# The first graph's set-up rebuilt in a graph network with experts, 16 graphs on one core

## The reference

```
H  = (adj != 0);  w = adj's first row
Be = 1 / column sums of H;  Dn = 1 / (H @ w)
conv(x, W, b) = Dn * (H @ (Be * (H.T @ (x @ W.T)))) + b
h  = relu(conv(layernorm(x), W1, b1))            # 512 wide
h  = layernorm(h) * gamma + beta
x1 = x + conv(h, W2, b2) + layernorm(x)          # 256 wide
x2 = layernorm(x1)
p  = softmax of the top 2 of 4 router logits of x2
e  = sum over experts of p * silu(x2 @ ew + eb)
y  = x2 + e @ ow + ob
out = x1 + nw * y / rms(y)
```

## Time and profile before

| what | value |
|---|---|
| time, median of 3 runs | 728.39 us (727.57 to 728.85) |
| the profiled execution's own time | 727.07 us |
| its span, first to last instruction | 725.5 us |
| TensorE busy | 685.5 us (94%) |
| VectorE busy | 622.0 us (86%) |
| ScalarE busy | 530.5 us (73%) |
| GpSimd busy | 345.2 us (48%) |
| the chain that ended last | PE 87%, DVE 5%, ACT 3% |

### The profile page before, as it was taken

One profiled execution on the slowest core, in us unless ns is written; L12 is line 12 of the kernel. 1 busy time (PEld: TensorE's weight loads), 2 busy tenths in 40 slices (PEclk: granted clock), 3 DMA queues, 4 the chain that ended last, 5 costly groups with the idle time before them and its releaser, 6 DMA issues.

```text
span 725.5 us, 15868 instructions
## 1 busy us (share of the span) xinstructions
PE 685.5 (94%) x5197; PEld 475.7 (66%) x5197; DVE 622.0 (86%) x1542; ACT 530.5 (73%) x1096; POOL 345.2 (48%) x732
## 2 busy tenths in 40 slices
PE   3777999999999999999999999999999999999973
PEld 2464485866758586775858577685857668585663
DVE  3987799898989989898989989898998989898676
ACT  4567868688696868778686877869686786967554
POOL 4142635456373545636354454635455463634444
PEclk9999999999999999999999999999999999999998
DMA  8547449375664938666583946657494756538312
GB/s 285 189 79 241 91 111 246 78 236 117 212 139 134 231 66 247 121 209 137 152 204 61 276 97 226 121 167 180 73 263 98 231 116 195 123 72 190 59 30 59
DMA packets 42590, 111.72 MB, mean 154 GB/s; under 512 B 4160, under 2 KB 5312, under 8 KB 42560
## 3 DMA queue, kind: packets, MB, share of 16 engines
q0 software_dynamic: 13536, 41.42, 32.5%
q1 hardware_dynamic: 29024, 69.92, 27.6%
HBM read 69.91 MB, written 16.25 MB: 119 GB/s over the span
## 4 chain that ended last, share of the span: by engine, by line
PE 87%; DVE 5%; ACT 3%; DMA 1%; issue 1%; POOL 1%; SPq 0%; POOLq 0%; DVEq 0%; ACTq 0%
PE bank L1335 16%; PE bank L1337 16%; PE bank L1336 16%; PE bank L1420 7%; PE bank L1421 7%; PE bank L1446 7%; PE bank L1478 4%; PE bank L1479 4%; PE bank L1389 4%; PE bank L1382 2%; PE bank L1437 2%; DMA b1b<-b 1%; PE bank L1491 1%; PE bank L1370 0%; ACT x L598 0%
## 5 line engine op out<-in xcount | busy, mean ns | idle before, releaser
L1335 PE MATMUL bank<-xth,ewh 128*128 128x512 f16 (+1 forms) x270 | 99.6, 369 | 2.6 <-DVE ewl L840 2.6
L1337 PE MATMUL bank<-xth,ewl 128*128 128x512 f16 (+1 forms) x270 | 99.8, 370 | 0.0
L1336 PE MATMUL bank<-xtl,ewh 128*128 128x512 f16 (+1 forms) x270 | 99.6, 369 | 0.0
L543 ACT ACTIVATE silu<-bank,ebcol,ksc 128x512 f32<-128x512 f32 x120 | 89.6, 768 | 7.7 <-POOL comb L400 3.9
L400 POOL TENSOR_TENSOR comb<-comb,silu 128x1024 f32<-128x1024 f32 x30 | 74.6, 2488 | 0.6 <-DVE silu L917 0.6
L1335 PE MATMUL bank<-w2h,hnth 128*128 128x256 f16 x256 | 70.3, 275 | 0.6 <-issue 0.6
L1336 PE MATMUL bank<-w2l,hnth 128*128 128x256 f16 x256 | 70.4, 275 | 0.0
L1337 PE MATMUL bank<-w2h,hntl 128*128 128x256 f16 x256 | 70.4, 275 | 0.0
L939 DVE SCALAR_TENSOR_TENSOR hntl<-bank,hnth 128x512 f16<-128x512 f32 x64 | 42.7, 687 | 26.6 <-ACT hnth L561 25.2
L1478 PE MATMUL bank<-xsh,h 128*128 128x256 f16 x256 | 59.4, 280 | 2.9 <-DVE xsl L822 2.3
L917 DVE TENSOR_TENSOR silu<-silu,bank 128x1024 f32<-128x1024 f32 x45 | 54.7, 1216 | 8.2 <-ACT silu L543 8.2
(11 more groups left out here) (283 smaller groups left out, 2077.1 us busy)
## 6 DMA issues: line engine op xcount, KB each, us to landing
adjin<-adj SPq DMA_DIRECT2D x16, 1024.0 KB, 5.4
adjtin<-adjt SPq DMA_DIRECT2D x16, 1024.0 KB, 8.2
xin<-x SPq DMA_DIRECT2D x16, 512.0 KB, 7.8
xb<-xn SPq DMA_DIRECT2D x16, 512.0 KB, 4.2
xb<-x POOLq DMA_DIRECT2D x16, 512.0 KB, 8.9
xb<-b POOLq DMA_DIRECT2D x16, 512.0 KB, 5.4
xb<-vadd POOLq DMA_DIRECT2D x16, 512.0 KB, 4.5
out<-x SPq DMA_DIRECT2D x15, 512.0 KB, 4.9
```

What stands on the lines that cost most here:

```text
L543: af(silu[:, i % 4, :], bank[E_BANK[i]][:, :], ACT.Silu, bias=ebcol[:, i:i + 1], scale=ksc[:, 2:3]).then_inc(silu_dn, 1)
L1335: mm(outp, lh, rh, start=first, stop=False)
L1336: mm(outp, lh, rl, start=False, stop=False)
L1337: return mm(outp, ll, rh, start=False, stop=last)
```

## The change

Loads: adj, W1 and adj transposed come right behind x; gamma, W2, beta and b1 follow as one group, and W1 has a semaphore of its own.

Magnitudes: ScalarE now writes the sum of the absolute values of a row straight into `mags` (`sum_abs`) for W1, gamma*W2 and the experts, in place of an absolute value whose maximum VectorE takes. VectorE takes the maximum itself for the two small matrices of group c. GpSimd multiplies gamma by W2.

Degrees: of graphs 0 and 1, TensorE adds them up by 16 products of H with a column of ones (`count_products`); graph 0's H transposed is one instruction of VectorE. From graph 2 on ScalarE counts them, as before.

Order in graph 0: x is normalised and split in two halves of two tiles, and A1 starts with the first half (`first_aggregation`); W1 is scaled before the second half of A1 is copied; Dn is computed before A2 is split; `beta_w2` follows the products with W1; GpSimd's `dnb` waits for group b apart from `dna`. TensorE multiplies zeros before its first real product (18 products of 512 columns) and between two transposes (twice 5), in `keep_busy`. Order in graph 1: the expert weights' halves are made earlier, those of the output weights later.

VectorE's program has 12 small memsets (`PAD`) in front of everything else. The loop's own code is as before except for the constants that the semaphores are compared with.

```diff
-            for dst, src in ((bet[:, :], beta), (gam[:, :], gamma),
+            sp.dma_start(adjin[:, :, :], adj[0].rearrange("(t p) e -> p t e", p=P)).then_inc(adj_in, 16)
+            sp.dma_start(w1f[:, :, :], w1t.rearrange("(k p) h -> p k h", p=P)).then_inc(a_in, 16)
+            sp.dma_start(adjtin[:, :, :], adjt[0].rearrange("(t p) c -> p t c", p=P)).then_inc(adjt_in, 16)
+            for dst, src in ((gam[:, :], gamma), (w2f[:, :, :], w2t.rearrange("(k p) f -> p k f", p=P)),
+                             (bet[:, :], beta), (b1b[:, :], b1.to_broadcast([P, DH]))):
...
+            gp.wait_ge(b_in, 64)
+            tt(w2g[:, :, :], w2f[:, :, :], gam[:, :].unsqueeze(2).to_broadcast([P, KH, D]), ALU.mult).then_inc(w2g_dn, 1)
...
+            def sum_abs(col, src):
+                n = src.shape[1] * src.shape[2]
+                return af(silu[:, :, :].rearrange("p k n -> p (k n)")[:, 0:n], src[:, :, :].rearrange("p k n -> p (k n)"),
+                          ACT.Abs, accum_out=mags[:, col:col + 1])
+
+            def first_x():
+                act.wait_ge(xrs_st, 4)
+                for j in range(2):
+                    s = slice(CG * j, CG * j + CG)
+                    for t in range(CG * j, CG * j + CG):
+                        af(xn[:, t, :], xin[:, t, :], ACT.Identity, bias=xnb[:, t:t + 1],
+                           scale=xrs[:, t:t + 1]).then_inc(xn_dn, 1)
+                    act.wait_ge(xn_dn, CG * j + CG)
+                    af(xsh[:, s, :], xn[:, s, :], ACT.Copy, scale=XS).then_inc(xs_hi if j else x0_hi, 1)
 
             def bias_rows(act, g):
...
+            for i in range(PAD):
+                v.memset(lead[:, i:i + 1], 0.0)
...
-            def first_ht():
-                dve.wait_ge(adjt_in, 16)
-                for t in range(CT):
-                    TS(ht16[0][:, t, :], adjtin[:, t, :], 0.0, None, ALU.not_equal, ALU.add,
-                       accum_out=deg[:, t:t + 1]).then_inc(ht_made, 1)
-                dve.wait_ge(ht_made, CT)
...
+            def first_lo(j):
+                s = slice(CG * j, CG * j + CG)
+                dve.wait_ge(xs_hi if j else x0_hi, 1)
+                STT(xsl[:, s, :], xn[:, s, :], XS, xsh[:, s, :], ALU.mult, ALU.subtract).then_inc(xs_lo if j else x0_lo, 1)
+
+            def setup_w1l(k):
+                dve.wait_ge(a_hi, 1)
+                STT(w1l[:, k, :], w1f[:, k, :], wsc[:, W1:W1 + 1], w1h[:, k, :], ALU.mult, ALU.subtract).then_inc(a_lo, 1)
...
+            def keep_busy(n):
+                for _ in range(n):
+                    mm(bank[7][:, :], m16[:, 0, :], m16[:, :, :].rearrange("p t c -> p (t c)"), start=True, stop=True)
+
+            def count_products():
+                for e in range(CT):
+                    for k in range(CT):
+                        ins = mm(bank[DEG_BANK][:, DEG][:, e:e + 1], h16[:, k, P * e:P * e + P], one16[:, :],
+                                 start=(k == 0), stop=(k == CT - 1))
+                ins.then_inc(deg_rdy, 1)
+
+            def first_aggregation():
+
+                def part(e, ks):
+                    b = bank[A1_BANK[e // CG]][:, D * (e % CG):D * (e % CG) + D]
+                    for k in ks:
+                        mm(b, h16[:, k, P * e:P * e + P], xsh[:, k, :], start=(k == 0), stop=False)
+                        ins = mm(b, h16[:, k, P * e:P * e + P], xsl[:, k, :], start=False, stop=(k == CT - 1))
+                    return ins
+
+                pe.wait_ge(x0_lo, 1)
+                part(0, (0, 1))
+                part(CG, (0, 1))
+                pe.wait_ge(xs_lo, 1)
+                part(0, (2, 3))
+                part(1, range(CT)).then_inc(a1_rdy, 1)
+                turn_mags(a_mag, 1, slice(W1, W1 + 1), 0, a_turn)
+                part(CG, (2, 3))
+                spread_max(a_top, 1, 0, a_max)
+                part(CG + 1, range(CT)).then_inc(a1_rdy, 1)
+
+            def first_product():
+                b = bank[A3_BANK[0]][:, :]
+                for k in range(KD):
+                    pe.wait_ge(a2_hi, k + 1)
+                    mm(b, a2h[:, k, 0:P], w1h[:, k, :], start=(k == 0), stop=False)
+                    pe.wait_ge(a_lo, k + 1)
+                    mm(b, a2h[:, k, 0:P], w1l[:, k, :], start=False, stop=False)
+                for k in range(KD):
+                    pe.wait_ge(a2_lo, k + 1)
+                    ins = mm(b, a2l[:, k, 0:P], w1h[:, k, :], start=False, stop=(k == KD - 1))
+                ins.then_inc(a3_rdy, 1)
 
             def a2_half(g, odd, half, ffn):
...
-                    setup_lo(c_hi, 2, ((rwf, rwh, rwl, RW), (owf, owh, owl, OW)), c_lo)
+                    setup_lo(c_hi, 1, ((rwf, rwh, rwl, RW),), c_lo)
...
+                    setup_lo(c_hi, 2, ((ewf, ewh, ewl, EX),), c_lo)
...
-                    setup_hi(c_scale, ((rwf, rwh, RW), (owf, owh, OW)), c_hi)
+                    setup_hi(c_scale, ((rwf, rwh, RW), (ewf, ewh, EX), (owf, owh, OW)), c_hi)
...
+            pe.wait_ge(tables, 12)
+            keep_busy(18)
```

More of the change, by code:

```diff
@@ L421, in body @@
                         root(hstat, hmv, hve, hrs, hnm, hnb, hrs_st, g, 16, 4 * t, slice(t, t + 1), 4, t + 1)
+                        if not ffn and t == 1:
+                            add_b2(g)
                 if ffn:
@@ L604, in body @@
                     a1_part(act, g, odd, 0)
+                if conv and not ffn:
+                    setup_hi(a_scale, ((w1f, w1h, W1),), a_hi)
                 if ffn:
@@ L608, in body @@
                     a1_part(act, g, odd, 1)
-                if conv and not ffn:
-                    setup_hi(a_scale, ((w1f, w1h, W1),), a_hi)
+                    if not ffn:
+                        act.wait_ge(a_mag, 1)
+                        act.wait_ge(w2g_dn, 1)
+                        sum_abs(W2, w2g).then_inc(b_mag, 1)
                 if ffn:
                     x2_part(act, f, 1)
-                if conv and ffn and not late:
-                    setup_hi(c_scale, ((ewf, ewh, EX),), c_hi)
                 if ffn:
@@ L658, in body @@
                     expert(act, f, 3)
+                if conv and not ffn:
+                    setup_hi(b_scale, ((w2g, w2h, W2),), b_hi)
                 if conv:
                     norm_h(act, g, 1)
+                if conv and not ffn:
+                    hnt_part(act, g, 0)
+                    relu(act, g, 3)
+                    hnt_part(act, g, 1)
                 if ffn:
@@ L695, in body @@
                         if e % CG == 0:
+                            if not ffn and e == 0:
+                                prep_x(g + 1, (0, 1))
                             act.wait_ge(u_rdy, 2 * g + e // CG + 1)
@@ L1062, in body @@
                 if conv and ffn:
-                    degrees(g, odd)
+                    degrees(g, odd, not late)
                 if ffn:
@@ L1097, in body @@
                 if conv and ffn and not late:
-                    setup_lo(c_hi, 3, ((ewf, ewh, ewl, EX),), c_lo)
+                    setup_lo(c_hi, 3, ((owf, owh, owl, OW),), c_lo)
                 if conv and ffn:
@@ L1463, in body @@
                 if conv:
-                    if not ffn:
-                        beta_w2()
                     pe.wait_ge(h_made, g + 1)
@@ L1469, in body @@
                         pe.wait_ge(y_dn, 2 * (g - 1))
-                    pe.wait_ge(xs_lo, g + 1)
-                    for e in range(CT):
-                        if ffn and e == 0:
+                    else:
+                        count_products()
+                    if not ffn:
+                        first_aggregation()
+                    else:
+                        pe.wait_ge(xs_lo, g + 1)
+                    for e in range(CT if ffn else 0):
+                        if e == 0:
                             pe.wait_ge(hnt_lo, 4 * g)
-                        if ffn and e == CG:
+                        if e == CG:
                             pe.wait_ge(u_lo, 4 * (g - 1) + 2)
@@ L1481, in body @@
                             ins.then_inc(a1_rdy, 1)
-                        if not ffn and e == 0:
-                            turn_mags(a_mag, slice(W1, W1 + 1), 0, a_turn)
-                    pe.wait_ge(ht_made, g + 4)
+                    pe.wait_ge(ht_made, g + 1)
                     pe.wait_ge(w_cur, g + 1)
@@ L1524, in body @@
                     if not ffn:
-                        pe.wait_ge(a_lo, 1)
-                    for t in range(CT):
+                        turn_mags(b_mag, 1, slice(W2, W2 + 1), 1, b_turn)
+                    if not ffn:
+                        first_product()
+                    for t in range(0 if ffn else 1, CT):
                         for k in range(KD):
@@ L1532, in body @@
                         ins.then_inc(a3_rdy, 1)
+                        if not ffn and t == 1:
+                            spread_max(b_top, 1, 1, b_max)
                         if ffn and t == 2:
@@ L1545, in body @@
                 if conv:
+                    if not ffn:
+                        beta_w2()
```

(4 more changed lines are left out.)

245 lines of the change are left out of this document (117 added, 128 removed).

## The result

| | before | after |
|---|---|---|
| median of 4 runs each, same chip | 727.98 us (727.52 to 728.85) | 715.42 us (714.63 to 715.79) |
| ratio of the two, 95% interval | | 0.9825 (0.9808 to 0.9842) |
| the profiled execution's own time | 727.07 us | 715.52 us |
| its span | 725.5 us | 714.0 us |

The forecast was 715.4 us, faster. The profiled executions differ by 11.55 us where I had forecast 13.0; the medians differ by 12.56 us. To about 1.5 us the agreement isn't luck.

A forecast was written before the change was run, and what follows sets the result against it. TensorE bounds the loop at 41.84 us per graph, so gains lie ahead of graph 2's D products: -6.7 -3.7 -3.3 -0.5 = -14.2 us, less 1.2 for handovers, -13.0: median 728.39 becomes 715.4 us, range 711.4 to 721.6.

The forecast's parts named there:

- First z: Start to graph 0's first z: 29.61 us becomes about 22.9 us, -6.7 us (bounds -3.5 and -8.5).
- The two costs that I had bounded: Graph 0's moved work: gamma*W2 on GpSimd, 2.5 us from about 16 us; VectorE's memsets, about 0.06 us each, costing nothing.
- z to D1: First z to the start of graph 1's D products: 31.25 us becomes 27.5 us, -3.7 us (bounds 0 and -4.5).
- D1 to the experts: Start of graph 1's D products to the first expert product: 9.93 us becomes 6.6 us, -3.3 us (bounds -1.0, -4.0).
- From there to D2: First expert product to the start of graph 2's D products: 38.41 us becomes 37.9 us, -0.5 us.
- The 1.2 us taken back for handovers: Deduction from the summed gain for some thirty handovers of 0.04 us rounded away: -14.2 us becomes -13.0 us.
- The first (the clock): TensorE's clock drops between zeros and A1, or again in a thin stretch of graph 0: 721.4 us, chance 0.12.
- The second: Loads come no earlier because DMAs share the engines in any order; costs 2.5 to 3 us: 718.2 us, chance 0.10.
- The third: Waits only move; VectorE becomes the bound in graph 0, second and third terms shrink to a third: 720.1 us, chance 0.09.
- the second term: The stretch from the first z to graph 1's D products, forecast 3.7 us shorter.
- The fourth: VectorE's loop stalls fetching code at each of six turns, 3 us per turn: 733.4 us, slower, chance 0.05.
- Decides from 2.2 us per turn: Stall per turn of VectorE's loop reaching TensorE at which six turns cancel the 13.0 us gain.

The follow-up runs named there:

- nozeros: The changed kernel without the 18 products of zeros at TensorE's start; 714.89 us, ratio 0.9809 to the kernel before.
- nofill: The changed kernel without the two groups of 5 products of zeros between graph 0's transposes; 715.53 us, ratio 0.9830 to the kernel before.
- pad44: The changed kernel with 44 memsets in front of VectorE's program instead of 12; 715.36 us, ratio 0.9835 to the kernel before.
- poolorder: The changed kernel with GpSimd's two additions of graph 0 (x, b2) moved behind the roots of h's tiles; 712.61 us, ratio 0.9796 to the kernel before.
- g1undo: The changed kernel with graph 1's order of expert and output weight halves as in the kernel before; 720.26 us, ratio 0.9896 to the kernel before.
- pad0: The changed kernel without the 12 memsets in front of VectorE's program; 746.85 us, ratio 1.0248 to the kernel before.

## Why the prediction was right, and where it was off

**What bounds it.** Right: TensorE's loop was untouched, and all of the gain lies ahead of graph 2's D products.

**First z, -6.7 us forecast, -5.8 measured.** H at 8.72 us (8.9 forecast) and W1's scale in the middle of A1 were as worked out. The D products were forecast at 16.2 us and came at 17.53, and this is the step that failed within the term: the zeros brought the rise of the clock, but it fell again in A1, 12.40 to 15.82 us. Where it didn't (six of the runs have them at 16.0 to 16.3 us) the step is right. From there to z 6.3 us, forecast 6.7. What z lost there is not in the time: D1 doesn't follow it (nozeros, nofill, pad44). The two costs that I had bounded are in the rows: gamma*W2 on GpSimd started at 15.06 us (16 forecast) and took 1.89 us (2.5), the memsets nothing.

**z to D1, -3.7 us forecast, -1.6 measured.** The largest miss. I counted VectorE's and TensorE's work and took GpSimd's roots as prompt. The change put `add_x` and `add_b2` in front of them, each with a wait for a DMA, and the sum has no term for these waits. poolorder gives 28.4 us for the stretch, against 29.7 in the changed kernel, 31.1 in pad44 with poolorder's z, and the 27.5 forecast. The half clock went, as forecast; the cost of `beta_w2` was 1.89 us and that of the fillers twice 1.24, 4.4 us together against 3.9 forecast.

**D1 to the experts, -3.3 us forecast, -3.1 measured** (9.93 to 6.85 us), and g1undo takes back 2.8 of it. **From there to D2, -0.5 us forecast, -1.2 measured** (38.41 to 37.26 us): the half clock is gone, and the wait for `a2l` that I had priced at 1.2 us is about 0.3 (the experts' last product starts at 62.72 us and the next one at 63.24, 0.22 us apart elsewhere).

**Sum.** Unrounded, -5.78 -1.58 -3.08 -1.15 is -11.6 us on the span, where -13.0 was forecast. The 1.2 us taken back for handovers made up for part of the miss, and no row prices them at 0.04 us each. Two slips changed little: 0.64, 0.12, 0.10 and 0.09 add up to 0.95, and the terms' stated bounds to -17 us at the far end.

**Rivals.** The first (the clock) happened in part, for 1.4 us at graph 0's D products, and cost nothing, since D1 was bound elsewhere. The second didn't: loads in order of use came earlier. The third is what shortened the second term, with GpSimd in VectorE's place. The fourth is real, and it is the reason for `PAD`: without it the rebuilt kernel stalls. I had given six turns of 3 us, 733.4 us; a loop of six passes turns back five times, it is 6.4 us each and 746.85 us. "Decides from 2.2 us per turn" was thus passed by far, and only the twelve memsets kept the loop off that place. The trace of before has no such turn to read it from.

**What the parts are worth**, each undone alone: the order in graph 1 3.1 us at D2 (its median is 4.8 us higher, on another chip), the sums of magnitudes 2.0 us at D2 (2.9 us against pad44, on the same chip), the loads about 1.5 us, not clear of the noise, the zeros nothing, and the memsets 31.4 us of time. If the parts add up, about 5 of the 11.6 us remain. I put them down to the order of graph 0 that no run undid (halves of x, degrees on TensorE, W2's scale behind z); that is not shown.

**Better than both**: poolorder, 712.61 us, 0.9796 (0.9775 to 0.9816). Its interval still touches that of the changed kernel (0.9808 to 0.9842); that the waits for h are gone and D1 moved by 2.8 us says more than the medians.

## What to carry to other kernels

Before putting an instruction with a DMA's wait ahead of others in an engine's order, list what stands behind it there: holding back GpSimd's small roots cost 2.8 us here, and TensorE's fillers hid part of it (nofill, without them, shows 1.09 us more of it as a wait for h). When an engine's program has a loop, look after every change, also one far ahead of it, at the turn (idle time put down to "issue") and at the count of code packets; if it stalls, a few cheap instructions in front move it. Value a filler only after the waits that it fills are gone.

## What of the hardware was not expected

- A loop on an engine can stall at each turn by its place in the program, with its code unchanged: VectorE's, with 316 or 444 instructions executed ahead of it, idles 5.4 and 6.8 us at a turn on average, 7.0 at most; with 322, 328, 329 or 360 not at all. Code packets are 8 KB each (0.32 MB in 39).
- After each such stall in pad0 TensorE is granted half its clock for 3.4 or 6.8 us although it had waited for VectorE 4.2 us at most, so that a turn costs 6.4 us, more than the idle time itself.
- The same program doesn't always get the same clock at its start: with the same 18 products of zeros, which took 5.36 us in the changed kernel and 7.00 in pad44, it rose at 5.6 us and fell at 12.40 in the first, and rose at 8.9 us and stayed up in the second. Graph 0's D products lie 1.4 us apart for it.
